# Adjacency loads that open 8 or 10 transfers later with six places in their ring, and half the software-DMA scratch, in a sparse graph-attention kernel

## The reference

```python
q, k, v = (x @ Wq + bq), (x @ Wk + bk), (x @ Wv + bv)      # split into 4 heads of 32
attn = einsum('nhc,mhc->hnm', q, k) / sqrt(32)
e = where(adj == 0, 0, exp(attn - rowmax over the edges)); alpha = e / sum(e)
out = einsum('hnm,mhc->nhc', alpha, v)
x_r = x @ Ws + bs
beta = sigmoid(concat(out, x_r, out - x_r) @ Wb)
y = layernorm(x + beta * x_r + (1 - beta) * out)
```

## Time and profile before

| | |
|---|---|
| median of 3 executions | 1904.53 us (1903.5 to 1909.21) |
| the profiled execution | 1922.68 us, its span 1920.8 us |
| VectorE busy | 1309.6 us (68%) |
| GpSimd busy | 1174.4 us (61%) |
| TensorE matmul busy | 1126.3 us (59%) |
| ScalarE busy | 838.8 us (44%) |
| moved by DMA | 438.72 MB, 228 GB/s in the mean |
| mean granted TensorE clock | 0.709 |

### The profile page before, as it was taken

The page is one execution under the profiler, slowest core; times in us unless marked ns, Lnnn a source line. Parts: engine busy times, 40 slices in busy tenths (PEclk is TensorE's granted clock), DMA queues, the critical chain, the costliest instruction groups (busy, mean ns, idle before and its releaser), DMA issues. The chain is left out here.

```text
span 1920.8 us, 20375 instructions
## 1 busy us (share of the span) xinstructions
PE 1126.3 (59%) x4636; PEld 657.7 (34%) x4696; DVE 1309.6 (68%) x3389; ACT 838.8 (44%) x1595; POOL 1174.4 (61%) x1711
## 2 busy tenths in 40 slices
PE   7322656666664655557656657775864655544553
PEld 5101333343342332324333324433432333333342
DVE  5877787786756677457756657757774577775564
ACT  2331442443643354345734537464753565431212
POOL 4365466656565566666566756666656655766664
PEclk9565776677776786767767767677776678675575
DMA  9956956776765676766876768777777677323321
GB/s 335 363 167 177 351 206 216 246 237 227 281 217 186 246 258 229 241 205 210 308 279 218 273 236 300 267 259 282 261 276 292 230 251 283 113 83 96 97 83 52
DMA packets 130040, 438.72 MB, mean 228 GB/s; under 512 B 26567, under 2 KB 61198, under 8 KB 97150
## 3 DMA queue, kind: packets, MB, share of 16 engines
q1 hardware_dynamic: 76510, 297.15, 42.0%
q0 software_dynamic: 52832, 136.07, 22.7%
q10 hardware_dynamic: 576, 4.19, 0.5%
HBM read 417.93 MB, written 19.44 MB: 228 GB/s over the span
## 5 line engine op out<-in xcount | busy, mean ns | idle before, releaser
L841 POOL DMA_INDIRECT s_kv<-kv_rows,s_rec_in x1023 | 1024.7, 1002 | 652.8 <-issue 394.6
L871 PE MATMUL s_ps_w<-s_mask,s_bit_w 128*128 128x512 bf16 x1003 | 368.6, 515 | 294.6 <-ACT s_mask L1065 204.3
L1065 ACT ACTIVATE s_mask<-s_adj_in 128x2048 bf16<-128x2048 f32 x252 | 478.3, 1900 | 106.0 <-DMA s_adj_in<-in_adj 68.6
L1043 PE MATMUL s_acc<-s_kv,ident 128*128 128x128 f32 x2032 | 301.6, 316 | 111.1 <-DVE s_kv L1314 70.0
L1043 PEld LDWEIGHTS s_acc<-s_kv,ident 128*128 128x128 f32 x2032 | 290.9, 230 | 137.6 <-DVE s_kv L1314 83.8
L871 PEld LDWEIGHTS s_ps_w<-s_mask,s_bit_w 128*128 128x128 bf16 x1008 | 109.9, 120 | 507.8 <-ACT s_mask L1065 254.4
L1288 DVE TENSOR_TENSOR s_kv<-s_kv,s_ps_q 128x1536 f32<-128x1536 f32 (+15 forms) x76 | 147.1, 1936 | 178.9 <-DMA s_kv<-kv_rows,s_rec_in 173.0
L1314 DVE TENSOR_TENSOR s_kv<-s_kv,s_ps_q 128x1536 f32<-128x1536 f32 (+15 forms) x76 | 146.7, 1931 | 9.5 <-ACT s_ps_q L1104 7.2
L1290 DVE TENSOR_REDUCE s_raw<-s_kv 128x48 f32<-128x1536 f32 (+15 forms) x76 | 147.1, 1935 | 5.6
L931 PE MATMUL s_ps_key<-s_d_kT,s_d_qT 32*128 32x512 f32 x128 | 101.9, 886 | 58.6 <-DVE s_d_pen L1505 41.7
L1092 ACT COPY s_xs<-s_ps_x 128x128 f32<-128x128 f32 x63 | 16.6, 264 | 258.9 <-remote 162.6
(11 more groups left out here) (281 smaller groups left out, 1511.5 us busy)
## 6 DMA issues: line engine op xcount, KB each, us to landing
s_adj_in<-in_adj SPq DMA_DIRECT2D x248, 1024.0 KB
s_kv<-kv_rows,s_rec_in POOLq DMA_INDIRECT x1023
kv_rows<-s_kv SPq DMA_DIRECT2D x16, 512.0 KB, 7.6
s_rec_in<-node_records SPq DMA_DIRECT2D x55, 106.0 KB
s_kv<-in_x_cols SPq DMA_DIRECT2D x4, 1024.0 KB, 8.3
s_adj_in<-in_adj ACTq DMA_DIRECT2D x4, 1024.0 KB
s_d_in<-in_x_cols SPq DMA_DIRECT2D x8, 512.0 KB
s_d_v<-kv_rows SPq DMA_DIRECT2D x8, 512.0 KB
```

Of the source, the lines that this page charges most:

```text
L841: nc.gpsimd.indirect_dma_start(out=kv[0:n, START[k] + s], out_offset=None, in_=kv_dram[:, :], in_offset=bass.IndirectOffsetOnAxis(ap=rec_i ...
L871: last = nc.tensor.matmul(w[:], bit_w[:, slab], mask[:, k % 2, s * WORD:(s + 1) * WORD], start=False, stop=(slab == SLABS - 1))
L1043: last = nc.tensor.matmul(acc[:, c * D:(c + 1) * D], ident[:], kv[:, START[k] + s, D:2 * D], start=(s == 0), stop=(s == plain(k) - 1))
L1065: nc.scalar.activation(mask[:, q % 2], adj_in[:, q % ADJ_RING], ACT.Sign, accum_out=edges[:, t, h:h + 1]).then_inc(masked, 1)
```

## The change

Three constants, and a semaphore less.

- The ring of adjacency parts has six places instead of five (8 KB more of each SBUF partition).
- LOAD_BEHIND, the number of transfers after FIRST_AT[k] at which the loads queued at unit k open, goes from 14, 14, 20, 20 to 22, 22, 30, 30. With six places the loads queued at unit k are q = 22 + 4k + j.
- The scratch that holds the descriptors of GpSimd's software DMAs is 8192 bytes of each partition; the default that the kernel had is 16384.
- The loop at the end that copies late rows counts on d_stored instead of on a semaphore of its own.

```diff
-ADJ_RING = PARTS + 1
+ADJ_RING = PARTS + 2
...
-LOAD_BEHIND = (14, 14, 20, 20)
+LOAD_BEHIND = (22, 22, 30, 30)
...
-        late_stored = sem("late_stored")
...
-                sp.dma_start(out[bass.ds(row, P), :], late_dram[bass.ds(row, P), :]).then_inc(late_stored, 16)
-                sp.wait_ge(late_stored, 16 * i + 16)
+                sp.dma_start(out[bass.ds(row, P), :], late_dram[bass.ds(row, P), :]).then_inc(d_stored, 16)
+                sp.wait_ge(d_stored, 16 * i + 32)
...
-    nc = _bacc.Bacc("TRN2", target_bir_lowering=False, num_devices=1)
+    nc = _bacc.Bacc("TRN2", target_bir_lowering=False, num_devices=1, dynamic_dma_scratch_size=8192)
```

## The result

The changed kernel takes 1877.35 us (median of 4, 1876.08 to 1882.01) against 1905.22 us of the kernel before beside it (median of 4, 1903.5 to 1909.21): ratio 0.9855 [0.9831, 0.9879], 27.9 us or 1.45% faster. The forecast was 1889.5 (1868 to 1915), faster. The sign, the range of 1868 to 1915 and the shorter pauses hold.

The account below looks back on a forecast made before the run. GpSimd was nearly always issuing or in a pause. Its lead of 35 us, less 20.5 at chunk 7, left 14.5; from the runs' median, 1904.5 - 15 = 1889.5 us, range 1868 to 1915, the forecast's own 1878 to 1899 (chance 0.46).

Parts of the forecast that it names:

- The pauses: GpSimd's 96 waits for a run's last gather to land: their sum falls by 35 to 45 us.
- X: GpSimd's lead over the kernel before at about 1476 us: 41 + 2.5 - 3 - 5 = 35 us.
- The small terms: GpSimd's new waits for late record loads: 4 us for tile 4 and 1 us for tile 8.
- What passes chunk 7: VectorE's lead after waiting for dense chunk 7's load, which lands 20.5 us later relative to GpSimd's transfers: 14.5 us.
- What of X reaches the end: VectorE carries 14.5 us to the end; GpSimd's surplus of 20 us is waited away at tile 48's record or unit 56.
- Half the scratch: GpSimd's descriptor scratch of 8192 bytes: no effect, taken as 0.
- rival C: All excess pause time in runs 7 to 74 goes: 30 to 40 us gained, 1868 us; chance 0.14.
- Rival A: Slower: later opening costs 20.5 us at dense chunk 7 and decides if X is smaller, 1913 or 1920 us; chance 0.22.
- margin of 10.7 us: GpSimd's margin at the slots of unit 56, given as 1547.8 - 1537.1.
- Rival B: No change: X between 15 and 26 cancels the later opening's cost, 1904 us; chance 0.16.
- Rival D: The scratch is too small, adding waits for landings worth 250 us: 2150 us; chance 0.02.
- estimate of 56 transfers: GpSimd's scratch of 8192 bytes holds 56 transfers, at nine descriptors of 16 bytes on each engine per transfer.

Follow-up runs that it names:

- second pair: The kernel before and the changed kernel, both unchanged, profiled again on one chip: profiled executions 1912.35 and 1879.06 us, ratio 0.9849.
- e1: Kernel before with LOAD_BEHIND (22, 22, 30, 30) alone, five places and the old scratch: ratio 0.999.
- e2: Changed kernel with the old LOAD_BEHIND (14, 14, 20, 20), keeping six places and the small scratch: ratio 0.997.
- before again: The kernel before, unchanged, profiled a second time on another chip: one execution, 1912.35 us.
- e5: Changed kernel with LOAD_BEHIND (26, 26, 34, 34): ratio 0.9849 to the kernel before.
- e3: Kernel before with the scratch of 8192 bytes alone: median 1916.99 us, ratio 0.998.
- e4: Changed kernel with the loads of dense chunks 4 to 7 ahead of the adjacency loads of the unit before: ratio 0.9877 to the kernel before.

## Why the prediction was right, and where it was not

*The pauses: right.* 35 to 45 us fewer were forecast, 38.5 and 38.0 are measured. The late ones of runs 7 to 52 went from 19 of mean 5.05 us to 4 of mean 4.1 (in the second pair from 13 of mean 5.65 to 4 of mean 4.03). All pauses of these runs fell by 37.1 and 34.4 us where 41 were forecast, those of runs 53 to 74 by 5.2 and 7.3 where 2.5 were. The 13 pauses of over 4.5 us that are left behind run 7 end runs with four adjacency loads in them, some with a dense chunk's loads beside, as before transfer 942 (5.62). Of the two edits, the opening makes the pauses short and the sixth place lets it be done without starving ScalarE (e1, e2). The prediction treated them as one and did not say that each alone is worth nothing. The Trainium skill's rule that it names for the long pauses ("DMA: Bandwidth & Descriptors", section on queues, rings and completion order), each DMA engine going round between its queues packet by packet, fits the delay that the rows show; no run here shows that it is the mechanism.

*X, GpSimd's lead at 1476 us: right.* 35 us forecast, 31 to 34 in the second pair. The small terms: tile 4's record 4 us forecast, 6.1 to 6.4 measured; tile 8's 1 us, 3.4 to 3.6.

*What passes chunk 7: right as a step.* 14.5 us forecast for VectorE, 12.6 measured.

*What of X reaches the end: wrong, in two sentences.* "It has no wait for gathers until after 1820, so it carries 14.5 us on and no more": it has no wait for gathers, but it has the wait for s_d_v behind it, 9.7 us at 1773 us already in the profile of before, whose load follows GpSimd's stores. I looked for the one kind of wait and not for all.

The other sentence is "GpSimd's surplus of 20 us is waited away", at tile 48's record: measured 0 and 0.77 us. The mechanism is there. In before again the last of the nine record loads left at 1591.9 and the gather that needs it at 1613.7; with the change these are 1578.3 and 1584.1, so GpSimd has come 16 us nearer to the record, and in e5 it waits 7.25 us for it. But the margin was read from an execution in which GpSimd already stood there 9.63 us, which it does not in before again, the one profile of that kernel without the stalls of the last section. With GpSimd's lead of 30 against VectorE's 14 the rows of before again would have said: a margin of some 16 us, just used up. So the last transfer goes by GpSimd's balance, 38.0 - 10.5 us and 2 us of smaller terms, 29.6, and not by VectorE's 14.5.

*Half the scratch: taken as 0, measured 3.7 us.* The rows on which that 0 rested were those of the transfers, which indeed did not change. The closing drain behind them was not looked at. With it the forecast would have been some 18 us; that the stated range held the time all the same it owes to rival C's end of it.

*Rival A* did not come, since VectorE's loss at chunk 7 ends at the loop's wait. At unit 56 TensorE's sum of unit 52 ended 5.5 us before the gather that takes its slots in the changed kernel (27.6 in before again), so it was close; in e1 it came. The prediction's margin of 10.7 us there was read to the end of that sum too; its first half is enough, so every such margin is some 2 us wider. *Rival B* needed an X of 15 to 26. *Rival C* came nearest in size (30 to 40 us against 27.9), with the wrong cause: not all excess went. *Rival D* did not come. The prediction's estimate of 56 transfers in 8192 bytes, worked out from what the Trainium skill states ("DMA: Bandwidth & Descriptors", section on the descriptor swizzle), stands against 12 in flight; e3, where nothing waits for room, agrees, and no run here shows where the scratch would become too small.

## What to carry to other kernels

Before saying that a delay on an engine reaches the end, list every wait of that engine behind it, of every kind: one wait for something that another engine's clock sets takes the delay away, and the end belongs to that other engine. When loads are moved later, name what stands behind them in the same queue (records, chunks) and move that ahead first: here that, with a still later opening, nearly doubled the gain. Two edits of which each gives nothing alone can be one change: a place in a ring is worth what the later opening can do with it. A stall that is in one profiled execution should be seen in a second before a margin is worked out from it. And a buffer's size can show at the very end of the program, behind the last piece of work: read the profile to its last row.

## What the runs showed of the hardware

**Engines that stand still on one chip and not on another.** The kernel before has two kinds of profile. In its first one, and in all four taken on the chip where it needs 1920.75 us (e1 to e4), ScalarE and TensorE stand idle again and again for 3 to 25 us with no releaser that the profile knows ("remote", or "issue" after a long gap). ScalarE's waits of the first profile of before and of e3:

```profile
ACT s_xs L1092 <- remote: 162.6, 22, 19.1
```

```profile
ACT s_xs L1092 <- remote: 147.7, 22, 14.2
```

In the eight other profiles there is not one such idle time of over 3 us on ScalarE. The windows of e3 around one of them (length, busy time and count of PE, PEld, DVE, ACT and POOL, granted clock, DMA share, GB/s), and two of the first profile after around the same step:

```profile
1482.00:1486.00 4.00, 1.14 (x5) 0.31 (x4) 3.69 (x11) 0.04 (x1) 3.06 (x3) 1.00 1.05 382
1486.00:1490.00 4.00, 0.00 (x0) 0.00 (x0) 0.43 (x1) 0.07 (x1) 3.05 (x3) 0.78 0.99 370
```

```profile
1467.00:1472.00 5.00, 5.00 (x41) 4.07 (x40) 4.26 (x14) 5.00 (x9) 3.78 (x5) 1.00 1.01 405
1472.00:1476.00 4.00, 4.00 (x15) 1.71 (x13) 3.69 (x9) 3.79 (x10) 3.08 (x4) 1.00 1.03 415
```

The DMA engines are full in both. In e3 TensorE and ScalarE do nothing from 1483 to 1490 although the transpose they need is shown done at 1481.1, and VectorE, which waits for them, stands 12.9 us; in the other nothing stands. GpSimd goes on through all of it. Many of the same lines stall at nearly the same times in before and e3 (505.7 and 505.9, 745.6 and 742.9, 1492.9 and 1489.9), so it goes at least in part with the place in the program. The kernel before has a median of 1920.75 us there and of 1905.8 and 1910.14 elsewhere; that the stalls make this difference is likely and not shown. What stops the engines is open. The traffic on the instruction queues is the same (84 and 38 packets), and in e3 none of their packets moved between 1474 and 1504 us, around the stall shown, so a packet of theirs in flight is not what the engines waited for there. No run here tried to tell more apart. The ratio of the change could not be compared there, since the changed kernel was not timed on that chip.

**The closing drain of GpSimd and the size of the scratch.** 9.85 us with 16384 bytes in three profiles, 5.12 with 8192 in e3, which differs from before in nothing else. It was 3.7 us of the kernel's time, since the end waited for it.

**A small gather's landing behind megabytes.** From the last gather's start to the next issue it is 3.6 us with nothing in the way and 6.9 to 8.5 us (pauses of 5.94 to 7.53) with two to four 1 MB loads issued shortly before; with the loads 15 us ahead it is 3.6 us again.
